# Cross attention: the order of ScalarE's exponentials and copies in the tile loop of a decoder kernel

## The reference

```python
q_r = jnp.einsum('bshq,hqr->bhsr', q_big, W_qr)          # queries after rope
k_r = jnp.einsum('bld,hdr->bhlr', kv_r, W_kr)            # keys: rotated context
scores = jnp.einsum('bhsr,bhlr->bhsl', q_r, k_r)
attn = jax.nn.softmax(scores, axis=-1)                   # over 1500 keys
ctx_c = jnp.einsum('bhsl,bld->bhsd', attn, kv_r)         # values: the same context
```

## Time and profile before

| what | value |
|---|---|
| median of 3 runs | 3228.09 us (3219.34 to 3236.89) |
| the profiled execution | 3207.39 us, its span 3205.4 us |
| PE busy | 2930.8 us, 91% of the span |
| DVE busy | 1877.8 us, 59% |
| ACT busy | 1242.9 us, 39% |
| POOL busy | 872.7 us, 27% |
| exponentials (L1795), each of three layers | 112, 1546 ns each |
| copies of turned probabilities (L1803), each of three layers | 112, some 571 ns each |

### The profile page before, as it was taken

The page is one execution under the profiler, slowest core; times in us unless marked ns, Lnnn a source line. Parts: engine busy times, 40 slices in busy tenths (PEclk is TensorE's granted clock), DMA queues, the critical chain, the costliest instruction groups (busy, mean ns, idle before and its releaser), DMA issues. The chain is left out here.

```text
span 3205.4 us, 48203 instructions
## 1 busy us (share of the span) xinstructions
PE 2930.8 (91%) x17997; PEld 1710.4 (53%) x17997; DVE 1877.8 (59%) x3657; ACT 1242.9 (39%) x1997; POOL 872.7 (27%) x743
## 2 busy tenths in 40 slices
PE   4889999979999989899999989989899999677999
PEld 3655555554455463355556557753355556346444
DVE  6558888833222257788885243347788885655222
ACT  3446666611111142456554122222456654524221
POOL 4324555400325024333333000004333333211000
PEclk8899999989999989999999999999999999888999
DMA  1147899723122212277876010012267875001111
GB/s 32 46 118 158 170 174 174 154 60 112 53 87 79 88 39 74 65 159 170 170 156 154 11 42 26 26 43 74 65 159 161 171 166 134 15 12 24 40 40 33
DMA packets 221444, 299.25 MB, mean 93 GB/s; under 512 B 127178, under 2 KB 149052, under 8 KB 218764
## 3 DMA queue, kind: packets, MB, share of 16 engines
q1 hardware_dynamic: 220348, 294.39, 39.4%
q10 hardware_dynamic: 864, 1.77, 0.2%
HBM read 120.52 MB, written 21.38 MB: 44 GB/s over the span
## 5 line engine op out<-in xcount | busy, mean ns | idle before, releaser
L1795 ACT ACTIVATE l1x_shared<-l1x_shared,l1x_a_low 128x1500 f32<-128x1500 f32 x112 | 173.1, 1546 | 157.6 <-DVE l1x_shared L1747 156.2
L1795 ACT ACTIVATE l2x_shared<-l2x_shared,l2x_a_low 128x1500 f32<-128x1500 f32 x112 | 173.1, 1546 | 157.1 <-DVE l2x_shared L1747 155.7
L1795 ACT ACTIVATE l0x_shared<-l0x_shared,l0x_a_low 128x1500 f32<-128x1500 f32 x112 | 173.2, 1546 | 132.6 <-DVE l0x_shared L1747 131.6
L2035 DVE TENSOR_TENSOR l0f_times_up<-l0f_gate,l0f_U 128x448 f32<-128x448 f32 x64 | 39.8, 621 | 236.9 <-PE l0f_U L1953 236.9
L1660 PE MATMUL l1x_a_S_ps<-l1x_kt,l1x_a_q 64*128 64x366 f32 (+1 forms) x896 | 176.7, 511 | 0.6 <-DVE l1x_shared L1747 0.6
L1660 PE MATMUL l0x_a_S_ps<-l0x_kt,l0x_a_q 64*128 64x366 f32 (+1 forms) x896 | 174.3, 506 | 3.1 <-issue 2.5
L1660 PE MATMUL l2x_a_S_ps<-l2x_kt,l2x_a_q 64*128 64x366 f32 (+1 forms) x896 | 176.5, 511 | 0.6 <-DVE l2x_shared L1747 0.6
L2004 ACT ACTIVATE l0f_gate<-l0f_G 128x448 f32<-128x448 f32 x72 | 39.1, 543 | 310.8 <-PE l0f_G L1948 310.8
L1353 POOL TENSOR_TENSOR l2x_q_straight<-l2x_q_straight,l2x_q_crossed 128x448 f32<-128x448 f32 x48 | 54.5, 1135 | 339.5 <-DVE l2x_q_crossed L1344 339.5
L1747 DVE TENSOR_SCALAR_CACHE_REDUCE l0x_shared<-l0x_a_S_ps 128x768 f32<-128x768 f32 x112 | 107.0, 956 | 64.8 <-PE l0x_a_S_ps L1660 62.2
L1695 PE MATMUL l1x_a_C_ps<-l1x_space,l1x_v 128*64 128x192 f32 (+1 forms) x1024 | 120.2, 369 | 11.8 <-DMA l1x_space<-l1x_a_blocks 9.6
(11 more groups left out here) (678 smaller groups left out, 6528.2 us busy)
## 6 DMA issues: line engine op xcount, KB each, us to landing
l0x_space<-normed SPq DMA_DIRECT2D x192, 128.0 KB
l1x_space<-normed SPq DMA_DIRECT2D x192, 128.0 KB
l2x_space<-normed SPq DMA_DIRECT2D x192, 128.0 KB
l0x_space<-l0x_a_blocks SPq DMA_DIRECT2D x186, 96.0 KB, 3.1
l1x_space<-l1x_a_blocks SPq DMA_DIRECT2D x186, 96.0 KB, 3.3
l2x_space<-l2x_a_blocks SPq DMA_DIRECT2D x186, 96.0 KB, 3.5
l0f_gu<-in_L_ffn_gu SPq DMA_DIRECT2D x36, 256.0 KB, 2.6
l0x_a_q<-l0x_qa SPq DMA_DIRECT2D x32, 224.0 KB
```

What stands on the lines that cost most here:

```text
L1795: act.activation(p[:, n % 2], p[:, n % 2], ACT.Exp, bias=low[:, n % 2, 1:2], scale=-1.0, accum_out=den[:, b % 2, k:k + 1]).then_inc(exp_re ...
L2035: dve.tensor_tensor(h[0:hid, g], a[0:hid, g], U[0:hid, 0:V], ALU.mult).then_inc(up_done, 1)
```

## The change

In ScalarE's loop over the tiles, the exponential of tile n + 2 is issued ahead of the copy of tile n and, in layer 0, ahead of the copies of the next keys. It was issued behind both.

```diff
                     if k == 6 and b > 0:
                         keep_contexts(b - 1, 1)
+                    if n + 2 < N:
+                        exp(n + 2)
                     keep(n)
                     if ctx is not None and k == 4 and b + 1 < B:
                         keep_keys(b + 1)
-                    if n + 2 < N:
-                        exp(n + 2)
```

## The result

The changed kernel is **slower**: 3292.6 us (median of 4 runs, 3283.0 to 3305.2) against 3227.7 us (4 runs, 3219.3 to 3236.9). The ratio is 1.0205 with a 95% interval of 1.0164 to 1.0246, that is +65 us where +59 was forecast. So the two profiles before and after, 98 us apart, show more than the change, and what is read from them is compared with the second.

The account below looks back on a forecast made before the run. TensorE, busy 91% of the span, was taken to bound the kernel, with ScalarE's order on the path only at layer 0's key transposes. Waits of 39 us plus 20 us of slow clock on 3228 gave 3287 us, range 3254 to 3306.

Parts of the forecast that it names:

- the likeliest case: Waits of 39 us plus 20 us of slow TensorE clock give 3287 us; chance 0.69.
- The waits at the key turn: Layer 0: next keys' transposes wait for tile 4's copy, 2.41 us later 14 times, 3.5 us in the first item.
- The clock: TensorE's clock falls after 13 of layer 0's 15 key transposes, 1.5 us each: 20 us.
- Steady tiles at nothing: Ordinary tiles of all three layers: the later copy still ends before the turn needing it, cost 0.
- the slack of 1.0 us: Steady tile: the turn could start at 1723.85 after the moved copy but starts at 1724.87.
- The earlier exponential collected by nobody: Layer 0, tile 6: exponential 2.14 us earlier, but its reader, the turn, starts much later, so nothing is won.
- Starts and ends: First and last tiles of the stages: extra waits for copies, 1.1 us at starts and 0.7 us at ends.
- The range: Whole kernel: 3254 to 3306 us, from waits alone to all 15 key turns slow, with measurement spread.
- A: Rival: layer 0's waits cost 39 us without any clock loss, 3267 us; chance 0.22.
- B: Rival: layer 0's earlier tile 6 exponential releases waiting work, up to 32 us back, about 3196 us; chance 0.02.
- C: Rival: layer 0's key transposes don't wait for tile 4's copy, only 2 us left, 3230 us; chance 0.04.
- D: Rival: steady slack is gone, up to 0.56 us in some 330 tiles, 185 us, 3470 at worst; chance 0.03.

Follow-up runs that it names:

- e1: New order in layer 0 alone, layers 1 and 2 as in the kernel before: 3273.5 us, ratio 1.0195 to the kernel before.
- e4: Changed kernel plus 12 unread TensorE matmuls in the wait ahead of each key transpose: 3251.7 us, ratio 1.0117 to the kernel before.
- e9: Changed kernel plus 9 unread TensorE matmuls in the wait ahead of each key transpose: ratio 1.0128 to the kernel before.
- e11: Changed kernel, unaltered, run once more on another chip for a second profile: 3263.4 us.
- e2: New order in layers 1 and 2 alone, layer 0 as in the kernel before: 3208.0 us, ratio 1.0000 to the kernel before.
- e6: New order in layers 1 and 2 alone, each copy of turned probabilities there made twice: 3204.6 us, ratio 0.9989 to the kernel before.
- e10: Kernel before, unaltered, run once more for a second profile; no total time is given, its layer 1 took 410.2 us.
- e8: Kernel before, with layer 0's next keys transposed ahead of tile 4's piece of the values: 3189.5 us, ratio 0.9933 to the kernel before.

## Why the prediction was right

- *Direction, size, place.* +59 us forecast, +65 measured (interval +53 to +79), all in layer 0. The number fell inside the range of the likeliest case.
- *The waits at the key turn* were forecast as 14 x 2.41 + 3.5 = 37.2 us. The profile has 2.33 to 2.34 us of idle at most of them, 2.38 us in an item that lost nothing else (e1), and in the first item the time from the first scores to the key transposes grew from 233.75 - 213.5 = 20.2 to 233.22 - 209.5 = 23.7 us, by 3.5. Right to a few per cent. e4, which has hardly any slow clock at the key turns, stands at +38 us, 6 of them its delay, and e9, which has less of it, at +41.
- *The clock* was forecast as 13 slow stretches at 1.5 us, 20 us. The count was right: 12, 14 and 13 of 15 in the three profiles with the wait unfilled (after, e11, e1). They cost more each. In e11 the 14 items take 58.2 us more than before; less 14 x 2.37 = 33.2 of wait and 2.8 of DMA waits, 22 us are the clock's. In that stretch 13 key turns are slow, and one, the first, was so before, so that is 1.8 us for each of 12. e4 won some 25 us with its delay and so 31 without, with the intervals of two ratios between them (some 10 us). So 22 to 31 us, a little above the forecast. The price was a single slow stretch as behind the DMA waits of the earlier trace rows; behind 6 of the 12 slow key turns of the first profile the slow time was at least twice that. That PE has idle time on both sides of the transposes there is a likely reason, which no run shows by itself. By the rule of the Trainium skill that was weighed there, that a wait between bursts makes the next burst start cold ("TensorE: Matmul & The Clock Gate", section "HAM oscillation — how this bites in real kernels"), all 15 would be slow. The traces agree in the main, with 39 of 45, but not turn by turn. The kernel that the section tells of waits 3 to 5 us for its DMAs, longer than the 2.3 us here, so it does not settle this case.
- *Steady tiles at nothing*: right (e2), and the slack of 1.0 us with it (e6).
- *The earlier exponential collected by nobody*: right. The turn that reads it waits for neither kernel's exponential, and no kernel with the new order was faster beyond its interval.
- *Starts and ends*, 1.8 us: too small to be measured here. The new waits of PE for copies in the first tiles are there (three of up to 1.35 us in layer 0, five in layer 1), and e2 shows no cost beyond its interval of 0.2%.
- *What the forecast lacked*: the waits for block DMAs in layer 0, about 6 to 9 us, counted as nothing. They can make up what lies between 59 and 65. The clock's term was too low as well, by 2 to 11 us, and the terms are known to some 10 us only (e4, e9), so it is partly luck that the total came so close.
- *The range.* Its upper end, 3306, is 3228 + 64.5 + 13; the upper bounds of start and end, which the text says it holds, are not in it and would make it some 3314. Nothing measured hangs on that.
- *Rivals.* A (waits without clock, 3267) fell by e4: the clock is worth some 25 us. B (faster) and C (no change) fell by the profile after, D (the steady slack) by e6.

## What to carry to other kernels

An instruction that is moved ahead on an in-order engine pushes back everything it is moved past; ask first who waits for *that*, and only then what the moved one wins. Here the copy was ready long before the exponential, and the exponential was not awaited by anybody. Idle time of TensorE in a dense stretch can cost more than itself: here 37 us of waits became some 60 with the slow clock behind them. Count the idle time on both sides of a short piece of work, and look in the trace before for a place that already has it. And where an engine has to wait for a hand-over anyway, put independent work between the two halves of it (e8) rather than in front.

## What the runs showed of the hardware

Key turns with a wait of TensorE of mostly 2.3 us, 0.86 us of transposes and 0.6 or 1.6 us of idle behind them lost the clock 39 times in 45 (12, 14 and 13 in 15), whereas the same transposes with that idle time behind them alone kept it in nearly all turns of the kernel before (all 14 of its profile, 13 of 14 in e10), and the same wait filled with 2.9 us of unread matmuls kept it 14 times in 15. Work whose result nobody reads made a kernel some 25 us faster than its like.
